# A new order of four engines' work in a fused graph attention and gated recurrent network kernel

## The reference

```python
h = jnp.maximum(_layernorm(x, axis=-1), 0.0)                # LN1
x = x + elu(softmax(where(adj > 0, leaky(e_i + e_j), NEG_BIG)) @ (h @ W))   # graph attention, e_i = h W a1, e_j = h W a2
h = jnp.maximum(_layernorm(x, axis=-1), 0.0)                # LN2, gives h0
for i in range(3):                                          # gated recurrent layers
    m = h @ weight[i]
    aggr = einsum('bst,bsd->btd', adj != 0, m)
    h = gru_cell(aggr, h)     # r, z: sigmoid; n = tanh(i_n + r * h_n); (1 - z) * n + z * h
x = x + h
```

## Time and profile before

| what | value |
|---|---|
| median of 3 runs | 742.43 us (742.2 to 743.38) |
| time of the profiled execution | 743.05 us |
| its span, first to last instruction | 741.2 us |
| mean granted TensorE clock | 0.953 |
| PE busy | 644.1 us, 87% |
| DVE busy | 533.8 us, 72% |
| ACT busy | 451.0 us, 61% |
| POOL busy | 288.5 us, 39% |
| one batch in the middle | 88.7 us |

### The profile page before, as it was taken

How to read it: one execution, slowest core, us unless ns; L and a number is a source line. 1 busy time by engine, 2 the same in 40 slices (tenths; PEclk the granted TensorE clock), 3 DMA queues, 4 the chain that set the end, 5 groups by cost and what they waited for, 6 DMA issues and landing times.

```text
span 741.2 us, 8817 instructions
## 1 busy us (share of the span) xinstructions
PE 644.1 (87%) x2845; PEld 474.4 (64%) x2845; DVE 533.8 (72%) x1218; ACT 451.0 (61%) x777; POOL 288.5 (39%) x295
## 2 busy tenths in 40 slices
PE   3587998979898998979889799897998979998996
PEld 2475756667575774658656586665756667666775
DVE  5768975669675795867947878567886679666444
ACT  2874866467774668556675576654857467754443
POOL 1104533335345153542623526325444335145442
PEclk9698999989999899999999899998999989999998
DMA  6421330113201231013310132012230113000101
GB/s 230 146 86 57 88 111 1 59 57 113 86 1 58 86 114 57 21 37 109 94 53 29 51 121 86 28 58 57 85 99 16 58 29 114 1 0 1 30 1 28
DMA packets 28670, 47.40 MB, mean 64 GB/s; under 512 B 1672, under 2 KB 19408, under 8 KB 28624
## 3 DMA queue, kind: packets, MB, share of 16 engines
q1 hardware_dynamic: 28624, 46.84, 19.9%
HBM read 42.60 MB, written 4.23 MB: 63 GB/s over the span
## 4 chain that ended last, share of the span: by engine, by line
PE 51%; DVE 21%; ACT 14%; POOL 7%; issue 6%; DMA 0%; DVEq 0%; POOLq 0%; ACTq 0%
PE ps_g L953 15%; PE ps_x L915 8%; PE ps_x L896 7%; ACT h_nat L350 3%; DVE hkT L724 3%; DVE nn L721 3%; DVE away L638 2%; ACT score L386 2%; DVE score L654 2%; PE ps_hn L896 2%; PE ps_x L936 2%; PE ps_r L963 2%; PE ps_r L964 2%; PE ps_r L962 2%; POOL zh L297 2%
## 5 line engine op out<-in xcount | busy, mean ns | idle before, releaser
L953 PE MATMUL ps_g<-edges,h_hi 128*128 128x512 f32 x384 | 163.1, 425 | 8.4 <-DVE h_lo L730 6.6
L953 PE MATMUL ps_g<-edges,h_lo 128*128 128x512 f32 x384 | 156.9, 409 | 0.0
L295 POOL TENSOR_SCALAR tz<-tz 128x512 f32<-128x512 f32 x48 | 29.7, 618 | 224.8 <-ACT tz L427 224.8
L386 ACT ACTIVATE score<-score,nmax 128x1024 f32<-128x1024 f32 x64 | 73.6, 1151 | 71.4 <-DVE nmax L654 71.3
L915 PE MATMUL ps_x<-probT,h_nat 128*128 128x512 f32 x224 | 99.4, 597 | 2.4 <-ACT probT L393 2.4
L953 PEld LDWEIGHTS ps_g<-edges,h_hi 128*128 128x128 f32 x384 | 77.1, 201 | 28.5 <-DVE h_lo L730 10.2
L896 PE MATMUL ps_x<-ident,score 128*128 128x128 f32 x512 | 72.6, 282 | 26.1 <-ACT aggT L401 15.1
L654 DVE CUSTOM_DVE_ANT_0 score<-score,away 128x1024 f32<-128x1024 f32 x64 | 89.2, 1394 | 7.8 <-ACT score L380 6.8
L896 PEld LDWEIGHTS ps_x<-ident,score 128*128 128x128 f32 x512 | 59.7, 145 | 42.4 <-ACT aggT L401 16.6
L953 PEld LDWEIGHTS ps_g<-edges,h_lo 128*128 128x128 f32 x384 | 76.7, 200 | 15.2
L393 ACT ACTIVATE probT<-ps_x 128x512 f32<-128x512 f32 x128 | 70.9, 596 | 13.3 <-PE ps_x L896 13.2
(11 more groups left out here) (133 smaller groups left out, 1331.6 us busy)
## 6 DMA issues: line engine op xcount, KB each, us to landing
adj_in<-in_adj SPq DMA_DIRECT2D x64, 512.0 KB, 3.3
x_nat<-in_x SPq DMA_DIRECT2D x8, 512.0 KB, 4.3
ej<-ej_kept_at SPq DMA_DIRECT2D x8, 512.0 KB, 3.6
out<-nn SPq DMA_DIRECT2D x16, 256.0 KB, 2.3
probT<-in_L_gnn_weight SPq DMA_DIRECT2D x1, 192.0 KB
probT<-in_L_gnn_w_ih SPq DMA_DIRECT2D x1, 192.0 KB
probT<-in_L_gnn_w_hh SPq DMA_DIRECT2D x1, 192.0 KB
ej_kept_at<-ej_row SPq DMA_DIRECT2D x8, 4.0 KB
```

Of the source, the lines that this page charges most:

```text
L386: act.activation(score[t % U][:], score[t % U][:], ACT.Exp, bias=nmax[:, t:t + 1], scale=-1.0, accum_out=rowsum[:, t:t + 1]).then_inc(exp_ ...
L953: last = pe.matmul(ps_g[c][:], part[:, s, :], edges[par][:, s, cols(c)], start=(s == 0 and part is h_hi), stop=(s == T - 1 and part is h_lo))
```

## The change

No instruction is added or taken away, except that `h_tiles` is cut into two halves of four. The orders of the five lists are changed:

- `rstd1(b + 2)` on POOL stands first in the body; it stood behind the splits of layer 0. The split of the first half of `h0T` stands last with the other one; it stood ahead of `z_times_h` of layer 2.
- `norm1(b + 2)` on DVE stands behind scores 1, ahead of `g_lo` of layer 0; it stood ahead of scores 4. `dots(b + 2)` stands behind scores 6, ahead of `lo_half` of layer 1; it stood ahead of `g_lo` of layer 2.
- `h_tiles(b + 2)` on ACT: half 0 ahead of exp 3, half 1 ahead of exp 6; all stood behind exp 6 and ahead of `aggT_half`.
- In layer 2 DVE does `n_input(2, 0)` ahead of the statistics of `x1`'s second half (`norm2`, split off `x1_half`), and `new_h(2, 0)` ahead of `n_input(2, 1)`. ACT does `hnb_half(2, 1)` ahead of `n_gate(2, 0)`.
- At the end of the body PE does the first transposes, eight neighbours, the other transposes, those of `h0`, and eight neighbours. Before, the sixteen neighbours stood behind all transposes (in body 6 ahead of them).

```diff
@@ gpsimd body
+                if prepare:
+                    rstd1(b + 2)
                 for l in range(L - 1):
...
-                    if prepare and l == 0:
-                        rstd1(b + 2)
                 if attend:
                     rstd2_half(b + 1, 0)
-                    split_h(b + 1, 0, 0)
                 z_times_h(b, L - 1, 0)
                 if attend:
                     rstd2_half(b + 1, 1)
                 z_times_h(b, L - 1, 1)
                 if attend:
+                    split_h(b + 1, 0, 0)
                     split_h(b + 1, 0, 1)
@@ scalar body
                     leaky_tile(a, a_par, 4)
+                if prepare:
+                    h_tiles(b + 2, par, 0)
+                if attend:
                     exp_tile(a, 3)
...
                     leaky_tile(a, a_par, 6)
+                if prepare:
+                    h_tiles(b + 2, par, 1)
+                if attend:
                     exp_tile(a, 6)
-                if prepare:
-                    h_tiles(b + 2, par)
-                if attend:
                     aggT_half(a, a_par, 0)
...
                 z_gate(b, 2, 0)
+                hnb_half(b, 2, 1)
                 n_gate(b, 2, 0)
-                hnb_half(b, 2, 1)
@@ vector body
                     scores(a, 1)
+                if prepare:
+                    norm1(b + 2, par)
                 g_lo_half(b, 0, 0)
...
-                if prepare:
-                    norm1(b + 2, par)
-                if attend:
                     scores(a, 4)
...
                     scores(a, 6)
+                if prepare:
+                    dots(b + 2, par)
                 if attend:
                     lo_half(b, 1, 0)
...
                     att_half(a, a_par, 0)
-                if prepare:
-                    dots(b + 2, par)
                 g_lo_half(b, 2, 0)
...
                     att_half(a, a_par, 1)
-                    x1_half(a, a_par, 1)
+                    x1_sum(a, a_par, 1)
                 n_input(b, 2, 0)
                 if attend:
+                    norm2(a, a_par, 1)
+                    new_h(b, 2, 0)
                     n_input(b, 2, 1)
-                    new_h(b, 2, 0)
@@ tensor body
                 gates_g(b, 2, 1)
-                if attend and not prepare:
-                    begin(a, a_par)
                 h_back(b, 2, 0)
                 if attend:
+                    neighbours(a, a_par, 0, 0, 0)
+                h_back(b, 2, 1)
+                if attend:
                     h0T_half(a, a_par, 1)
-                h_back(b, 2, 1)
-                if prepare:
-                    begin(a, a_par)
+                    neighbours(a, a_par, 0, 0, 1)
```

More of the change, by code:

```diff
@@ L279, in rstd1 @@
                 if b > 0:
-                    pool.wait_ge(h_done, b)
+                    pool.wait_ge(h_done, b * 2)
                 rstd_of(rstd[:], shift[:], mv, T, b + 1, vare_done, pow_done, rstd_done)
@@ L343, in _, with h_tiles @@
         def _(act):
-            def h_tiles(b, par):
+            def h_tiles(b, par, c):
                 act.wait_ge(rstd_done, b + 1)
@@ L348, in h_tiles @@
                     act.wait_ge(agg_ps, b * 2 - 2)
-                for t in range(T):
+                for t in range(c * TH, (c + 1) * TH):
                     last = act.activation(h_nat[par][:, t, :], x_nat[par][:, t, :], ACT.Relu, bias=shift[:, t:t + 1],
@@ L441, in first @@
             def first():
-                h_tiles(0, 0)
+                h_tiles(0, 0, 0)
+                h_tiles(0, 0, 1)
                 row_of_ej(0, 0)
@@ L451, in first @@
                     if t == 2:
-                        h_tiles(1, 1)
+                        h_tiles(1, 1, 0)
+                        h_tiles(1, 1, 1)
                     if t == TH + 2:
@@ L622, in dots @@
             def dots(b, par):
-                dve.wait_ge(h_done, b + 1)
+                dve.wait_ge(h_done, b * 2 + 2)
                 if b == 0:
@@ L670, in x1_half, with x1_sum @@
             def x1_half(b, par, c):
+                x1_sum(b, par, c)
+                norm2(b, par, c)
+            def x1_sum(b, par, c):
                 n = b * 2 + c + 1
@@ L679, in x1_half, with norm2 @@
                                          ALU.add).then_inc(x1_done, 1)
+            def norm2(b, par, c):
+                n = b * 2 + c + 1
                 dve.wait_ge(x1_done, n)
```

## The result

The changed kernel takes 709.61 us (median, 708.97 to 710.96) against 742.32 us: 0.9566 of the time before, with a 95% interval of 0.9538 to 0.9595. That is 32.7 us less; the forecast was 706 us, in a range of 692 to 724.

What follows compares the result with a forecast made beforehand. PE, busy 87% of the span, was taken as the bound, with its waits and clock to win. 24 + 10 + 4.2 - 2 - 0.3 = 36 us off 743.05 gave 707, by the median 706 us; range 692 to 724.

Steps and rivals of the forecast that it cites:

- ends and heads, bodies 0 to 5: Earlier body ends less what the next heads give back: 10 us for five heads, 4.2 us where body 6 follows.
- end of body 6: Half the neighbours moved behind the transposes leave PE as late as DVE's hkT makes it: minus 0.3 us.
- head of body 0: Body 0 has the new norm1 without an earlier end of a body before it: minus 2 us.
- Term 1: Layer 1, h_tiles and norm1 moved: waits for aggT, g_lo, probT vanish, plus 0.4 for restarts; 4.0 us per body, 24 us.
- Term 2: End of a body, four edits together: hkT comes earlier and PE ends at 338.2 instead of 342.96, 4.8 us.
- the time of half 1: End of a body: hkT of half 1 ends at 331.5, against 332.72 before, after rstd of 2.2 us on POOL.
- The chapter on POOL against DVE: Rule against the change: a split on POOL costs DVE 0.5 to 0.9 us at its place, perhaps its whole length.
- with the slow clock gone: End of a body: no wait longer than 2.52 us is left, so no slow clock; otherwise some 2.9 us less gain.
- the 4.8 us: PE's gain at the end of a body, of which 3.1 us were to stay at the next products of g.
- A clock of 0.50 behind the new waits: Sign that the forecast is wrong: granted clock at the 1.2 GHz level behind PE's new waits.
- That gap did not bring the slow level: Layer 1: after PE's wait of 2.52 us the four transposes take 0.66 us and not 1.11.
- The head: Start of the next body: norm1 waits for x_nat, so PE starts g at 342.8; 2.0 us kept in each of five heads.

Runs made afterwards that it cites:

- the run with the preparation only: Changed kernel with the end of the body put back on all four engines; rstd1, norm1, dots and h_tiles stay in new places: 711.46 us.
- the filled kernel before: Kernel before, with eighteen useless matmuls in PE's wait of 4.66 us ahead of the first transposes, bodies 0 to 5: 734.66 us.
- `n_gate` first: Changed kernel with ACT's n_gate of half 1 ahead of the four tiles of h0's second half in layer 2: 703.97 us.

## Why the prediction was right, and where its steps were off

The forecast was 36 us and 32.7 were measured. That the sum came so near is in part luck: one term was 5.5 us too small and two were 6 and 3 us too large. By the spans, which differ by 32.0 us:

| term | forecast | shown |
|---|---|---|
| layer 1, six bodies (norm1 and h_tiles away) | 24 | 29.5 in the run with the preparation only: 4.5 in each of five bodies, 7.0 in body 0 |
| ends and heads, bodies 0 to 5 | 14 | 8: from 86.48 to 621.27 before, 88.69 to 585.93 after, makes 37.5, less the 29.5. With the old end (preparation only, 88.86 to 590.46) it is already 3.7, so the new end has 4.4 of the 8 |
| end of body 6 | -0.3 | -3.3 |
| head of body 0 | -2 | -2.2 |

**Term 1** had the mechanism right. PE's waits for `aggT`, `g_lo` and `probT` are gone, and `dots` and the halves of `h_tiles` fit into idle places of DVE and ACT. The waits were sized right too: 3.6 forecast, 3.55 us less idle time of PE in a body. What was too small is the 0.4 us for the restarts, which no row stood behind: PE's busy time fell by 0.95. I put it down to the restarts; no run tests that. In body 0 the trace of before had also a slow stretch, behind its wait for `aggT`, that is gone: 7.0 us and not 4.5. `norm1` alone gave PE all of its 2.2 us and not the 1.1 of `g_lo` and `probT`, since `aggT` came 0.6 us earlier as well; but that 0.6 was already in the 2.5 of the sum.

**Term 2** failed at one step, the time of half 1: "New: 325.4 + 2.2 + 4.2 = 331.8 ... I take 331.5". `hkT` of half 0 came at 326.3 and not 326.9, which is close. `hkT` of half 1 came at 332.8, 1.3 us later than the sum. Rstd took 2.95 us on POOL, not 2.2, beside DVE's instructions, and the split which I had moved on paper out of the way of half 0 stood exactly beside `hkT` of half 1 and cost it 0.95 us. The chapter on POOL against DVE had the price of this (0.5 to 0.9 us, by the row of another `hkT`), but I charged it to the scores only. The Trainium skill, page "SBUF — State Buffer", section "Who interferes with whom", says that a DVE instruction with two SBUF inputs contends with a GpSimd one that reads SBUF, and that the shared port pair is an exclusive lock. This row agrees: `hkT` began 0.5 us behind POOL's instruction and ended 0.55 us behind it, nearly its own 0.69 us.

The wait left over was therefore 4.0 us and not 1.5 (by the sum's own numbers, 326.9 + 2.5 against 331.5, it should have read 2.1), and the step "with the slow clock gone" fell with it: from the transposes of half 1 to the score tile it took 8.0 us (316.84 to 324.85) and not 6.7. So of the 4.8 us, 1.4 are lost as PE takes up half 1 later and 1.3 at the slow clock. "A clock of 0.50 behind the new waits" was among the signs of being wrong, and it came: from 317.90 to 320.90 the granted clock is 0.50. Useless matmuls in that wait bring the clock back and 4.5 us with it. "That gap did not bring the slow level", said of the wait of 2.52 us, was read from one body. In body 0 of the same trace the same wait brought it (0.79 above), as it did in all bodies of the run with the new end alone and in four of the filled kernel before.

**The head** gave back nothing at that place: PE's 2.1 us were still there at the product of g. SP issued the load of x at 336.2 by the old trace's time (320.16) and not 335.6, and DVE waited 0.8 us for it (1 to 2 were forecast). PE did not wait for `g_lo`; because the 4.8 us were only 2.1, it came at 343.9 and so later than the limit that I had worked out at 342.8. The limit was reached as soon as PE was made faster (1.06 and 1.59 us), and it then held back most of what that won in bodies 0 to 4. A little further on some of the 2.1 us goes back all the same: from the product of aggT with w to the first neighbours of layer 1 it is 35.55 us (302.04 to 337.59) where it was 37.05 (318.07 to 355.12), 1.5 us less, behind a wait of 0.35 us for `hkT` of layer 0 that was not there before. The swap on ACT was priced at nothing; it was not tried alone.

**Body 6** was mis-sized. I wrote that PE is as late as DVE's `hkT` makes it, and took 0.3. From the first neighbours of layer 1 in body 6 to those in body 7 it took 77.15 us before (621.27 to 698.42) and takes 80.43 now (585.93 to 666.36). Changed kernel:

```profile
647.93 0.66 PE L909 MATMUL ps_r<-ident,hkT 128*128 128x128 f32 x4 [4.01 <-DVE hkT L737]
...
666.36 0.50 PE L966 MATMUL ps_g<-edges,h_hi 128*128 128x512 f32 x1 [1.42 <-DVE h_lo L743]
```

Before, the sixteen neighbours stood ahead of the transposes, inside a wait; eight of them, 1.9 us, now stand behind `hkT` of half 1. And the clock in the 8 us behind the wait is 0.79 where it was 1.00; with the useless matmuls in the wait it is 1.00 again, and the stretch takes 78.83 us. But PE's old order is no cure by itself. The run that has it puts sixteen neighbours ahead of the transposes in body 6 too, and takes 80.08 us there (593.85 to 673.93): PE waits 2.29 us for `hkT` of half 1, and then for `h_lo`, where the kernel before waited 0.23 and 0.41 us:

```profile
658.23 0.79 PE L966 MATMUL ps_g<-edges,h_hi 128*128 128x512 f32 x1 [1.76 <-DVE h_lo L713]
```

With `n_gate` first, and PE's new order kept, it takes 77.60 us. A kernel with all four old orders in body 6 alone was not tried.

Whether the moved parts add up was not a question in the prediction, and it should have been: the end of the body is worth +1.2 us alone and -1.9 us behind the preparation, both hardly more than the noise, and each of its parts undone singly costs 2.5, 6.8 and 8.5 us. By the traces this comes from two kinds of waits, one that is handed on to the next releaser and one behind which the clock falls.

## What to carry to other kernels

Work taken off the list of an engine that feeds another one can be worth its full length, and more than the waits that the profile puts down to it: `norm1` was 2.2 us, and the waits for DVE's `g_lo` and ACT's `probT` behind it 1.1. Count the cost of a restart as well, and take it from rows. Look at a wait in every body before you say what the clock does behind it. Work that is moved to the end of a list is not out of the way; look for what runs beside it there, above all on DVE and POOL. And before a gap of PE is priced, count with the clock behind it, and behind the other gaps: a gap closed in one place can bring the slow clock in another, so parts of one change are measured together and apart.

## What the runs showed of the hardware

The same wait of PE was followed by different clocks, also within one execution of one kernel. Over the 8 us behind it, 4.7 us gave 0.66 and 0.80 in the run with the preparation only; 2.5 us gave 0.79 in body 0 of the kernel before and 1.00 in its bodies 1 to 5, and 0.79 in all six bodies with the new end alone. A wait of 1.9 us gave 0.79 in one body of the run with `norm1` only and 1.00 in the others. Which of the two it will be could not be read from the length of the wait; what decides it stays open here. Useless matmuls in the wait kept the clock behind it at 1.00 in both kernels in which this was looked at.

A VectorE instruction that takes 0.69 us alone took 1.64 us beside a GpSimd one. That was so for two different GpSimd instructions, and each time it ended 0.54 or 0.55 us behind the GpSimd one.
